# A LoRA projection in four batches instead of five: twelve weight shares moved to VectorE, and the first down stage reordered

## The reference, cut to what matters

```python
def _qlora_linear(x, wq, A, B):
    w = jnp.tile(wq, (1, 4))
    base = x @ w.T
    lora = x @ A.T @ B.T
    return base + lora * 0.5
gate = silu(_qlora_linear(x, w1q, a1, b1)); up = _qlora_linear(x, w3q, a3, b3)
ffn = _qlora_linear(gate * up, w2q, a2, b2)      # rank 2, hidden 2752, d 1024
xn = layernorm(x)                                # 4096 tokens x 1024
out = x + autocorrelation_mix(xn) * silu(ffn)
```

## Time and profile before

| what | value |
|---|---|
| median of 3 runs | 840.47 us (838.67 to 840.76) |
| profiled execution: its time, its span | 841.09 us, 839.3 us |
| PE busy | 823.3 us (98%) |
| PEld, DVE, ACT, POOL busy | 52%, 70%, 39%, 18% |
| PE in the chain that ended last | 91% of the span |
| PE's waits over 0.3 us after the first 25 us | one, 1.8 us, ended at 72.67 us |
| mean granted clock of TensorE | 0.997 |

### The profile page before, as it was taken

How to read it: one execution, slowest core, us unless ns; L and a number is a source line. 1 busy time by engine, 2 the same in 40 slices (tenths; PEclk the granted TensorE clock), 3 DMA queues, 4 the chain that set the end, 5 groups by cost and what they waited for, 6 DMA issues and landing times.

```text
span 839.3 us, 11191 instructions
## 1 busy us (share of the span) xinstructions
PE 823.3 (98%) x4168; PEld 439.4 (52%) x4168; DVE 585.1 (70%) x949; ACT 330.7 (39%) x542; POOL 149.2 (18%) x242
## 2 busy tenths in 40 slices
PE   5999999999999999999999999999999999999997
PEld 4443575345844467334763347534585345844366
DVE  7888854696776876688667786678776696744535
ACT  5986645434133342332423342333423434132231
POOL 5324101222012220122201230023201222000000
PEclk9999999999999999999999999999999999999999
DMA  9822026000240003300042010501015000220004
GB/s 283 306 85 76 26 102 226 26 26 25 82 146 26 26 26 126 101 26 26 27 154 72 26 34 18 201 25 51 26 52 176 26 0 1 102 101 1 0 2 151
DMA packets 19190, 63.17 MB, mean 75 GB/s; under 512 B 2496, under 2 KB 4256, under 8 KB 18864
## 3 DMA queue, kind: packets, MB, share of 16 engines
q1 hardware_dynamic: 19120, 62.33, 21.5%
HBM read 45.54 MB, written 16.78 MB: 74 GB/s over the span
## 4 chain that ended last, share of the span: by engine, by line
PE 91%; DVE 3%; ACT 2%; issue 2%; DVEq 1%; POOL 1%; DMA 1%; SPq 0%; ACTq 0%; POOLq 0%
PE g L1292 26%; PE u L1292 24%; PE g L1506 5%; PE u L1506 5%; PE zb L1447 4%; PE u L1515 4%; PE g L1515 4%; PE g L1513 4%; PE u L1513 4%; PE g L1343 3%; PE mb L1376 1%; PE g L1509 1%; PE u L1509 1%; ACT w_sq L568 1%; DVEq L903 1%
## 5 line engine op out<-in xcount | busy, mean ns | idle before, releaser
L568 ACT ACTIVATE sil<-g,winv 128x512 f32<-128x512 f32 (+1 forms) x176 | 119.9, 683 | 271.2 <-PE g L1343 241.3
L887 DVE SCALAR_TENSOR_TENSOR h<-u,winv,sil 128x512 f32<-128x512 f32 x168 | 125.7, 749 | 115.0 <-ACT sil L568 99.2
L1292 PE MATMUL g<-xt,w_h 128*128 128x512 f16 x656 | 196.8, 382 | 0.0
L1292 PE MATMUL u<-xt,w_h 128*128 128x512 f16 x656 | 195.7, 380 | 0.0
L1292 PE MATMUL g<-xt,w_l 128*128 128x512 f16 x328 | 124.8, 381 | 0.0
L1292 PE MATMUL u<-xt,w_l 128*128 128x512 f16 x328 | 124.6, 380 | 0.0
L830 DVE CUSTOM_DVE_ANT_0 junk<-xn,abc 128x1024 bf16<-128x1024 f32 x96 | 120.3, 1253 | 5.6 <-issue 2.2
L1292 PEld LDWEIGHTS u<-xt,w_h 128*128 128x128 f16 x656 | 64.4, 98 | 78.0 <-issue 1.1
L1292 PEld LDWEIGHTS g<-xt,w_h 128*128 128x128 f16 x656 | 55.5, 98 | 84.2 <-issue 33.8
L465 POOL TENSOR_TENSOR ve<-mv,three 128x1 f32<-128x1 f32 x30 | 6.7, 223 | 468.8 <-DVE mv L812 468.8
L1038 DVE SCALAR_TENSOR_TENSOR ob<-xr,c_mean,gg 128x1024 f32<-128x1024 f32 x27 | 34.6, 1283 | 56.4 <-ACT gg L568 36.0
(11 more groups left out here) (259 smaller groups left out, 1138.6 us busy)
## 6 DMA issues: line engine op xcount, KB each, us to landing
xr<-in_x SPq DMA_DIRECT2D x32, 512.0 KB, 4.7
out_x<-ob SPq DMA_DIRECT2D x31, 512.0 KB, 2.9
xf<-in_x SPq DMA_DIRECT2D x30, 512.0 KB, 3.2
raw_w<-in_w2t SPq DMA_DIRECT2D x1, 2560.0 KB
abc<-in_a SPq DMA_DIRECT2D x1, 2048.0 KB, 7.8
raw_w<-in_w1t SPq DMA_DIRECT2D x2, 768.0 KB, 8.1
raw_w<-in_w3t SPq DMA_DIRECT2D x2, 768.0 KB, 9.5
base_b<-in_w2t SPq DMA_DIRECT2D x2, 512.0 KB, 4.7
```

Source lines behind the costliest of these rows:

```text
L568: return nc.scalar.activation(out, in_, f, **kw)
L887: stt(out=h[0:n, p % NH, :], in0=up, scalar=winv[0:n, 3 * block_of(p) + 1:3 * block_of(p) + 2], in1=sil[0:n, p % 2, :], op0=ALU.mult, op1= ...
L1292: o = mm(bank[:], a, x, start=opens and t == 0, stop=closes and t == len(terms) - 1)
```

## The change

Now every chunk is a base chunk, and the tail too. Pairs 0, 4, 8, 12, 16 are left out of the batches, and the tail pair 21 is joined with 20 (JOINT): 32 of its rows are copied by ACT into pair 20's slot once the first tail sum has read it. 16 pairs are left, which are four batches (at pairs 7, 12, 17 and in the down stage). `add_base` is called for six chunks and two ranks: 12 times instead of 4. Six of these are in group 0's pairs, six in its down stage. `w2_high` of chunks 3 to 5 moves behind the tail work on ACT, and all six `w2_low` to the end of VectorE's tail work. In group 0 TensorE now runs `down_high` of tile 1 ahead of the last batch, and of tile 2 ahead of `down_low(0)`; in groups 1 to 7 all five chunks of tile 0 go ahead of the batch.

```diff
-BASE = (3, 4)
-Z_PAIRS = tuple(p for p in range(NP_) if p not in [4 * n for n in BASE])
+NBASE = HN + 1
+JOINT = 4 * HN
+Z_PAIRS = tuple(p for p in range(JOINT) if p % 4) + (JOINT,)
...
+        base_b1 = sb("base_b1", [P, L], F32, at=o_at + 4096)
...
-        W2L_AT = {19: 0, 20: 1}
-        BASE_AT = {10: (0, 0), 12: (1, 0), 17: (0, 1), 18: (1, 1)}
-        Z2_AT = {5: 0, 9: 1, 13: 2, 19: 3}
+        BASE_AT = {10: (0, 0), 16: (0, 1), 17: (1, 0), 18: (1, 1), 19: (2, 0), 20: (2, 1)}
+        C_LOADS = 13
+        Z2_AT = {7: 0, 12: 1, 17: 2}
...
-        W2_AT = {13: 0, 15: 1, 16: 2, 19: 3, 20: 4, 21: 5}
+        W2_AT = {18: 0, 20: 1, 21: 2}
...
@@ SP: raw_a2 and base_a in 11 transfers instead of 1 @@
-            for buf, name in ((raw_a2, "a2t"), (fwd, "fwd"), (inv, "inv")):
+            a2 = d["a2t"]
+            sp.dma_start(raw_a2[:, 0:JOINT, :], a2[:, 0:JOINT, :]).then_inc(c_loaded, 16)
...
+            for buf, name in ((fwd, "fwd"), (inv, "inv")):
...
+                    if i == 0:
+                        sp.wait_ge(b_rest_done, 4)
+                        sp.dma_start(base_b1[:], d["w2t"][97, HN, :].partition_broadcast(P)).then_inc(base1_loaded, 16)
                     front_load(i + 1, 3)
...
@@ ACT, tail_shifts @@
-                A(half_b[0:32, :], h[32:64, LAST % NH, :], ACT.Copy).then_inc(shift_done, 1)
-                act.wait_ge(half_done, at_group(i, 2, 2))
+                act.wait_ge(half_done, at_group(i, 2, 1))
+                A(h[0:32, JOINT % NH, :], h[32:64, LAST % NH, :], ACT.Copy).then_inc(shift_done, 1)
                 A(half_b[0:32, :], half_a[32:64, :], ACT.Copy).then_inc(shift_done, 1)
...
@@ ACT, w2_high @@
-                if n in BASE:
-                    act.wait_ge(base_done, 2 + BASE.index(n) + 1)
+                act.wait_ge(base_done, 2 * n + 2)
...
@@ ACT, main loop @@
                 tail_shifts(i)
+                if i == 0:
+                    w2_high(3)
                 folded_high(i, HN)
...
                 z2_copies(i)
                 if i == 0:
+                    w2_high(4)
+                    w2_high(HN)
+                    b2_high()
                     second_z()
...
@@ DVE, tail_sums @@
+                if i == 0:
+                    add_base(3, 0)
+                    add_base(3, 1)
                 dve.wait_ge(shift_done, at_group(i, 3, 2))
...
-                if i == 0:
-                    w2_low(3)
...
@@ DVE, main loop @@
-                        if p == 9:
+                        if p == 6:
                             half_base()
...
                 folded_low(i, HN)
                 if i == 0:
-                    w2_low(HN)
-                    w2_tail()
+                    add_base(4, 0)
+                    add_base(4, 1)
                     dve.wait_ge(zeroed, 10)
                 z2_stack(i)
                 if not last:
                     xt_low(i + 1, 0)
                     xt_low(i + 1, 1)
+                if i == 0:
+                    add_base(HN, 0)
+                    add_base(HN, 1)
+                    for n in range(HN + 1):
+                        w2_low(n)
+                    w2_tail()
...
@@ PE, z2 @@
+                if n == ZB - 1:
+                    pe.wait_ge(shift_done, at_group(i, 3, 2))
...
@@ PE, main loop @@
                 if i == 0:
                     down_high(0, range(0, 3))
+                    down_high(1, range(0, 3))
                     z2(0, ZB - 1)
                     xt_across(1)
                     second_scale()
                     down_high(0, range(3, HN))
-                    down_high(1, range(0, HN))
+                    down_high(1, range(3, HN))
                     second_z0()
+                    pe.wait_ge(xtl_done, 4)
+                    down_high(2, range(0, HN))
                     down_low(0)
                     second_spread()
                     down_low(1)
+                    down_low(2)
                     pe.wait_ge(zst_done, 2)
                 else:
-                    down(i, 0, range(0, 3))
+                    down(i, 0, range(0, HN))
                     z2(i, ZB - 1)
...
```

More of the change, by code:

```diff
@@ L289, in build @@
         a2_done, a2_diff, zeroed = sem("a2_done"), sem("a2_diff"), sem("zeroed")
-        base_loaded, base_done = sem("base_loaded"), sem("base_done")
+        base_loaded, base1_loaded = sem("base_loaded"), sem("base1_loaded")
+        base_done = sem("base_done")
         stats_done, dev_done, normed = sem("stats_done"), sem("dev_done"), sem("normed")
@@ L419, in _ @@
                     block_load(b, m)
-            for buf, name in ((raw_a2, "a2t"), (fwd, "fwd"), (inv, "inv")):
+            a2 = d["a2t"]
+            sp.dma_start(raw_a2[:, 0:JOINT, :], a2[:, 0:JOINT, :]).then_inc(c_loaded, 16)
+            sp.dma_start(raw_a2[32:P, JOINT, :], a2[32:P, JOINT, :]).then_inc(c_loaded, 16)
+            sp.dma_start(raw_a2[0:32, JOINT, :], a2[32:64, LAST, :]).then_inc(c_loaded, 16)
+            sp.dma_start(raw_a2[0:32, LAST, :], a2[0:32, LAST, :]).then_inc(c_loaded, 16)
+            for rows in (32, 64, 96):
+                sp.dma_start(raw_a2[rows:rows + 32, LAST, :], a2[0:32, JOINT, :]).then_inc(c_loaded, 16)
+            for rows in (0, 64):
+                for part in range(2):
+                    sp.dma_start(base_a[rows + 32 * part:rows + 32 * part + 32, HN, :],
+                                 a2[0:32, JOINT + part, :]).then_inc(c_loaded, 16)
+            for buf, name in ((fwd, "fwd"), (inv, "inv")):
                 sp.dma_start(buf[:], d[name]).then_inc(c_loaded, 16)
@@ L544, in _ @@
                 raw_difference(q)
-            pool.wait_ge(c_loaded, 16 * 3)
-            for n in BASE:
+            pool.wait_ge(c_loaded, 16 * C_LOADS)
+            for n in range(HN):
                 tt(raw_a2[:, 4 * n + 1:4 * n + 4, :], raw_a2[:, 4 * n + 1:4 * n + 4, :],
                    raw_a2[:, 4 * n:4 * n + 1, :].broadcast_to([P, 3, 2]), ALU.subtract).then_inc(a2_diff, 1)
-            pool.wait_ge(a2_diff, len(BASE))
+            tt(raw_a2[:, JOINT, :], raw_a2[:, JOINT, :], raw_a2[:, LAST, :], ALU.subtract).then_inc(a2_diff, 1)
+            pool.wait_ge(a2_diff, NBASE)
             for u in range(3):
@@ L779, in _ @@
                         folded_high(i, p // 4 - 1)
-                    if i == 0 and p == LAST:
-                        b2_high()
                 tail_shifts(i)
+                if i == 0:
+                    w2_high(3)
                 folded_high(i, HN)
@@ L852, in half_base, with add_base @@
             def half_base():
-                dve.wait_ge(c_loaded, 16 * 3)
-                for k, n in enumerate(BASE):
-                    ts(base_a[:, k, :], raw_a2[:, 4 * n, :], 0.5, None, ALU.mult)
-            def add_base(k, row):
-                n = BASE[k]
+                dve.wait_ge(c_loaded, 16 * C_LOADS)
+                for n in range(HN):
+                    ts(base_a[:, n, :], raw_a2[:, 4 * n, :], 0.5, None, ALU.mult)
+                ts(base_a[:, HN, :], base_a[:, HN, :], 0.5, None, ALU.mult)
+            def add_base(n, row):
                 dve.wait_ge(w2_loaded, 16 * 7)
-                dve.wait_ge(base_loaded, 16 * (row + 1))
                 if row:
-                    dve.wait_ge(base_done, k + 1)
-                stt(out=raw_w2[:, n, :], in0=base_b[:], scalar=base_a[:, k, row:row + 1], in1=raw_w2[:, n, :],
-                    op0=ALU.mult, op1=ALU.add).then_inc(base_done, 1)
+                    dve.wait_ge(base1_loaded, 16)
+                    dve.wait_ge(base_done, 2 * n + 1)
+                else:
+                    dve.wait_ge(base_loaded, 16)
+                stt(out=raw_w2[:, n, :], in0=(base_b, base_b1)[row][:], scalar=base_a[:, n, row:row + 1],
+                    in1=raw_w2[:, n, :], op0=ALU.mult, op1=ALU.add).then_inc(base_done, 1)
             def lag_gap(i):
@@ L1630, in _ @@
                         xt_across(i + 1)
-                    down(i, 0, range(3, HN))
                     down(i, 1, range(0, HN))
@@ L1634, in _ @@
                     down(i, 1, range(HN, HN + 1))
-                if not last:
+                if i and not last:
                     pe.wait_ge(xtl_done, 2 * i + 4)
-                down(i, 2, range(0, HN + 1))
+                if i:
+                    down(i, 2, range(0, HN + 1))
                 if i and not last:
```

20 lines of the change are left out of this document (6 added, 14 removed).

## The result

| | before | after |
|---|---|---|
| median, us (range) | 840.11 (838.67 to 840.76) | 846.66 (844.63 to 847.59) |
| ratio of the runs (95% interval) | | 1.0082 (1.0070 to 1.0094) |
| profiled execution: time, span | 841.09, 839.3 | 844.63, 842.5 |
| four executions after: time (mean granted clock) | | 844.63 (0.998), 846.35 (0.994), 846.98 (0.994), 847.59 (0.992) |

The kernel is slower by 6.55 us, where I forecast 3.1, and the median lies 0.16 us over the range of 8 in 10. (The median before is 840.11 with a fourth execution; the forecast started from three and 840.47.) The profiled execution is near where the forecast put it: span 842.5 for 842.4. That agreement is in part luck, since a clock term too high by 1.7 and a term of groups 1 to 7 too low by 1.35 cancel in it.

The account below looks back on a forecast made before the run. TensorE was taken as busy all the time, so its time is run time. -6.8 - 0.9 - 1.7 + 9.1 + 1.7 + 1.7 = +3.1, taking the median from 840.47 to 843.6; range of 8 in 10: 839.3 to 846.5.

Parts of the forecast that it names:

- the range of 8 in 10: Whole kernel: the time forecast to lie, 8 times in 10, between 839.3 and 846.5 us.
- The clock: Group 0's down stage: 1.7 us lost behind each of the two longer waits, bounds 0 and twice that.
- Groups 1 to 7: Each loses one batch of 0.97 us and TensorE has no new wait: gain 6.8 us.
- The batch's cover: Last batch in groups 1 to 7: ScalarE's copy into pair 20's slot comes 1.8 us before TensorE needs it.
- Pair 5: Group 0: the batch there goes, but its 0.97 us becomes a wait; nothing gained.
- Pair 14 and up to T: Group 0 before T (LoRA matmuls of pairs 20, 21): wait halves, gain 0.9 us, plus 1.7 of clock.
- The stage: Group 0's down stage: TensorE waits 1.5 us at chunk 2, 4.9 at chunk 4, 2.7 ahead of tile 3; 9.1 together.
- T + 10.35: When TensorE would reach tile 0's fifth chunk without the first wait, counted from the LoRA matmuls of pairs 20, 21.
- The sum: Whole kernel: all gains and losses together make +3.1 us, median 840.47 to 843.6.
- the third case of the prediction: Rival: clock slower than taken, also at pair 14, or one fall lasting twice as long; 845.3 to 847 us; chance 0.17.

Follow-up runs that it names:

- e12: Changed kernel with one of VectorE's last four projections of groups 1 to 6 put between its two tail sums: 844.79 us, ratio 1.0059.
- e4: Changed kernel with the last batch and next group's transposes behind four chunks of tile 0 instead of five in groups 1 to 7: 848.89 us, ratio 1.0108.
- e2: Changed kernel with tile 2's high and low passes of group 0 back behind the spread of z: 846.18 us, ratio 1.0087.
- e3: Changed kernel with VectorE's branch of group 0 ahead of the sums for z's second block: 843.92 us, ratio 1.0053.
- e7: Kernel before the change with four added TensorE waits of 2.0 us in group 7: 852.05 us, ratio 1.0131.
- e8: Kernel before the change with four added TensorE waits of 4.8 us in group 7: 868.77 us, ratio 1.0347.
- e11: Kernel before the change with four added TensorE waits of 0.8 us in group 7: 842.45 us, ratio 1.0043.

## Why the prediction was wrong, step by step

- **Groups 1 to 7: -6.8 forecast, -5.45 measured** (the end from group 0's last matmul on). A missed term, and the first step that failed. From batch to batch a group became shorter by 100.38 - 99.65 = 0.73 us, where I took 0.97. I named what is late next only for the batch itself. z2's sum comes 10.52 us behind the start of the stage (216.90 - 206.38, with one batch less ahead of the stage), 9.61 before, and the chain behind it on DVE, four projections, branch, first output, ends in ScalarE's read of tile 1, which PE needs for tile 3. e12 took this wait away. The batch's cover, which I put at 1.8 us, is close to nothing (e4). I had left DVE's first tail sum where it stood in the trace of before. But with a batch less ahead PE reaches the stage earlier and DVE does not: the sum starts 211.22 - 206.38 = 4.84 us behind the stage's start now, and 202.52 - 198.89 = 3.63 before. That is 1.21 us later, where a batch is 0.97. Before, the stage started with

```profile
198.89 0.58 PE L1506 MATMUL g<-w_h,hf_h 128*128 128x512 f32 x1
```
- **Pair 5: nothing gained**: right, a wait of 1.13 (forecast 1).
- **Pair 14 and up to T: -2.6 forecast, -2.74 measured.** The wait is 0.54 (0.9 forecast), and a new one of 0.65 us, at 57.88 for DVE's product, was not forecast. Up to pair 14 PE is 72.67 - 71.56 = 1.11 ahead, and the other 1.63 come between there and T, where the fall is missing: in this execution both terms came out. The eleven small transfers took SP 0.4 to 1.0 us each and delayed nothing.
- **The stage: waits of 1.5 + 4.9 + 2.7 = 9.1 forecast, 1.88 + 5.11 + 2.43 = 9.42 measured**, in their places and with their releasers. Right. (The terms up to the fifth chunk, 1.4 + 5.6 + 2.26 + 0.94, make T + 10.2 and not T + 10.35, so the second wait should have read 5.0.)
- **The clock: the second step that failed, with pair 14 worth as much as the first.** "I take 1.7 for each of the two", and -1.7 at pair 14. In the profiled execution only one fall came, so the forecast span was met with one term too high (1.7) and one too low (1.35). The median is another matter. Five traces have the stage's first two waits of the changed kernel (its own, e2, e3, e4, e12). Behind the first a fall came in two of the five, and shortened the second wait; behind the second one fall in the changed kernel's own trace and two in each of the other four; behind the third (own, e4, e12) in two of three. By the windows the second wait lost 1.7, 2.3, 3.4, 3.1 and 3.3 us, 2.8 on the mean, and the third 2/3 x 1.7 = 1.1. That is 3.9 us, where I took 3.4 and where this execution shows 1.7. And the 1.7 us at pair 14 were worth less: the kernel before lost them in its profiled execution, 841.09, which lies 0.98 over its median. Of the four traces with that wait at 1.8 us (its own, e7, e8 and e11) two have a fall behind it, so the mean gain is about half of 1.7.
- **The sum.** 844.63 - 841.09 = 3.54 between the two profiled executions, 0.98 from there to the median of before, 846.66 - 844.63 = 2.03 to that of after: 6.55. The first is near the forecast, with its two errors cancelling; the other two are what single executions differ by. Taken from means, the 3.45 us that the forecast lacks are 1.35 from groups 1 to 7, 0.85 from pair 14, 0.5 from the clock in the stage and 0.3 from its waits. The 0.4 us left are within the interval of the ratio (1 us on each side).

So the time lies where the third case of the prediction had it (the clock costs more than taken, 845.3 to 847), to which I gave 0.17. Its words "also at pair 14 ... or one fall lasting twice as long" are both what some executions show, but the clock by itself explains only some 1.4 us; without the missed term of groups 1 to 7 the median would have been in the range. Not settled is which of the falls each of the untraced executions had; their mean clocks only give the count.

The clock's term was open to a better bound in the trace of before. One fall behind 1.78 us, at the one place where PE waited, bounded nothing from above for a wait nearly three times as long; the upper end of the range, 2.9 us over the forecast, left room for one more fall of 1.7 and not for two.
